# A decoder layer on one core: the same 4459 steps, written out in another order

## The chip, the core and the metric

One core of a Trainium2 chip runs the whole program. It has five engines with a queue each: TensorE (PE, matmuls; its weight loads are listed as PEld), VectorE (DVE), ScalarE (ACT), GpSimd (POOL), and SyncE (SP), which here only issues DMAs. Semaphores order them. The metric is the device time of one execution in microseconds, as the median over runs. Beside it stand times of one profiled execution, in which every instruction has a start and a duration; its span goes from the first to the last instruction.

## The reference

Sixteen samples (`x` is 16 x 512 x 256) go through one decoder layer in float32. Nothing passes from one sample to another.

```python
def attn(h):                      # 16 heads of 16, 64 landmarks
    q, k, v = heads(h @ Wqkv + bqkv);  q = q * scale
    q_l, k_l = mean8(q), mean8(k)      # 8 rows to a landmark
    attn1, attn2, attn3 = softmax(q @ k_l.T), softmax(q_l @ k_l.T), softmax(q_l @ k.T)
    V = attn2
    for _ in range(6):
        KV = attn2 @ V
        V = 0.25 * V @ (13*I - KV @ (15*I - KV @ (7*I - KV)))
    return attn1 @ (V @ (attn3 @ v)) @ Wout + bout
x = x + attn(layernorm(x))
x = x + cross_attention(layernorm(x), ctx, mask)   # 64 keys, 16 heads
h = layernorm(x)
e = argmax(gelu(h[:, -1] @ Wp1 + bp1) @ Wp2 + bp2) # one expert of 8 for each sample
x = x + h + 0.3 * ((gelu(h @ W1[e] + b1[e]) @ W2[e] + b2[e]) @ Wo + bo)
```

(The last line is written as the kernel has it: `h + 0.3 * out` is what the expert layer returns.)

## The kernel before

The work is cut into steps. A step is one engine's share of one operation of one sample, from one to about 30 instructions, with one increment of that engine's semaphore at its end. A word such as `P.jT.1-2` names it: engine (P, A, D, G for POOL, S for SP), kind, part, and how many samples behind the newest one it works. `TURN` lists the steps of one turn; `program()` unrolls it over 16 samples, so that a turn works on four or five samples at once, and `LAST` lists the last steps one by one, with the sample behind `@`. `PROGRAM` is that list. Each engine executes its own steps in the list's order, and waits only for the steps that its data or its buffers need (`unmet`). The eight PSUM banks are given out in the same order (`plan()`): a matmul step takes the bank that has been free longest, and waits for the step that emptied it. So the list alone decides the order on each engine, and which bank each step waits for.

Kinds that matter here:
- `xnTa`, `xnTb`, `xnTc` transpose the normalised input of the three parts; `q`, `k`, `v` project; `s2`, `s3`, `s1`, `t1` are scores of the first attention, `sx`, `tx` of the second; `mx3`, `mx1`, `mxx` their maxima on DVE; `e3`, `e1`, `ex` their exponentials on ACT; `den`, `o`, `w` the sums, the weighted values and the output projection, with `1` or `x` behind; `rec` the reciprocals.
- One of the six rounds of the inverse: PE's `iT` and `iZ` (L1133), from which DVE makes `wb` and ACT `az`; then PE's `jT` and `jZ` (L1143), from which DVE makes `ut` and `uz`, and POOL from `ut` the `b7` for the next `iT`.
- `gate`, `logit`, `exp` choose the expert and load its weights; `h` and `y3` compute it.
- Only once, for sample 0: `w2`, `f` and `fb` multiply each expert's second matrix with the output matrix and store the result; `cn` loads 16 constants; `cst` makes constants on POOL; `kx` computes all keys of the cross attention.

PE works with four shapes of its array: the full 128 x 128 (projections, transposes, experts), 64 x 64 (the inverse and `a`, `x2T`, `y`), 32 rows by 128 columns (all scores), and 128 rows by 32 columns (`den`, `o`, `zT`); `vx` takes 128 by 64. A neighbouring pair of steps in different shapes is called a switch here, and a run of steps in one shape a group.

A wait for a bank and the 64 x 64 matmuls read so:

```python
for j in range(banks_of(step)):
    if BEFORE[i, step, j]:
        who, i0, emptier = BEFORE[i, step, j]
        if c := unmet(pe, who, i0, emptier):
            pe.wait_ge(done[who], c)
```

Of the kernel before, what the change touches and what calls it, by code (L numbers as in the profile page):

```python
# [13 lines left out]
P = 128  # L14
# [16 lines left out]
    D.wb.5.0-3 P.h.2-4 G.kbd-2 D.s2-2 P.jZ.5-3 A.f.2-1 D.uz.5.1-3 D.uz.5.0-3 D.rec1.1.1-3 P.h.1-4 P.y-3
    P.s3.0-2 A.h.2-4 D.y-3 P.o1.0-3 P.o1.1-3 D.rec1.0.1-3 D.o1.0-3 D.o1.1-3 D.mx3.0.0-2 D.mx3.0.2-2
    A.e2-2 P.h.3-4 A.e3.0.0-2 D.mx3.0.3-2 D.mx3.0.1-2 P.w1.1-3 A.e3.0.2-2 D.soft2-2 D.w1.1-3 A.e3.0.3-2
    A.e3.0.1-2 P.w1.0-3 D.w1.0-3 P.f.1-1 P.f.7-2 D.lnB-3 G.xr-2 A.h.1-4 A.f.7-2 S.x-1 G.lnB-3 P.h.0-4
    P.p3T.0-2 P.p3T.3-2 P.p3T.2-2 P.p3T.1-2 A.h.0-4 A.p3T.0-2 A.p3T.1-2 P.x2T-2 S.f.5-3 P.s3.1-2 A.x2T-2
    A.p3T.2-2 A.h.3-4 D.mx3.1.3-2 D.mx3.1.1-2 A.p3T.3-2 P.a.0-2 A.e3.1.3-2 A.e3.1.1-2 P.a.1-2 P.zT.0-2
    D.mx3.1.2-2 D.mx3.1.0-2 P.kx.0-2 P.y3.1-4 A.a.0-2 P.p3T.7-2 P.p3T.5-2 A.e3.1.2-2 A.e3.1.0-2 S.f.1-2
    G.b7.0.0-2 P.p3T.6-2 A.zT.0-2 P.p3T.4-2 P.xnTb.0-3 A.a.1-2 D.lnA-1 G.b7.0.1-2 A.p3T.7-2 S.w2.6-1
    P.xnTb.1-3 D.kx.0-2 A.p3T.5-2 P.f.5-2 A.p3T.6-2 G.x1b-3 A.p3T.4-2 P.fb A.xnTb.0-3 P.s1.0-2
    A.xnTb.1-3 A.f.5-2 D.y3.1-4 P.zT.1-2 P.iT.0-2 A.zT.1-2 D.mx1.0.0-2 S.w2.3-1 P.qx.0-3 G.lnA-1 P.z-2  # L40
    P.f.0-1 S.cn-1 D.mx1.0.2-2 P.f.3-1 D.wb.0.1-2 A.qx.0-3 D.mx1.0.3-2 P.qx.1-3 A.qx.1-3 D.z-2 P.kx.1-2
    D.mx1.0.1-2 D.wb.0.0-2 P.sx.0-3 D.mxx.0.1-3 D.kx.1-2 P.sx.1-3 D.nmA-1 D.mxx.0.3-3 D.mxx.0.0-3
    P.y3.0-4 D.mxx.1.2-3 S.w2.5-1 D.mxx.1.3-3 D.mxx.1.1-3 P.iZ.0-2 A.az.0.0-2 D.mxx.1.0-3 D.mxx.0.2-3
    A.f.1-1 P.xnTa.1-1 A.az.0.1-2 A.xnTa.1-1 A.f.0-1 D.mpx-3 S.f.6-3 P.xnTa.0-1 D.y3.0-4 A.xnTa.0-1
# [30 lines left out]
    A.e1.1.3@14 D.uz.2.1@14 D.lmq.0@15 P.iZ.3@14 A.q.1@15 P.iT.3@14 A.az.3.0@14 D.lmq.1@15 A.az.3.1@14
    P.v.0@15 D.wb.3.0@14 G.qbd@15 D.wb.3.1@14 P.jT.3@14 D.v.0@15 P.jZ.3@14 D.ut.3.0@14 P.s2@15
    D.ut.3.1@14 G.b7.4.0@14 D.uz.3.0@14 D.uz.3.1@14 G.b7.4.1@14 P.s3.0@15 D.s2@15 P.iZ.4@14 D.mx3.0.0@15
    P.iT.4@14 A.az.4.0@14 A.az.4.1@14 P.v.1@15 D.mx3.0.1@15 A.e2@15 D.wb.4.0@14 A.e3.0.0@15 D.wb.4.1@14
    D.mx3.0.2@15 A.e3.0.1@15 P.jT.4@14 D.mx3.0.3@15 P.jZ.4@14 A.e3.0.2@15 D.ut.4.0@14 P.p3T.1@15
    D.ut.4.1@14 G.b7.5.0@14 A.e3.0.3@15 D.uz.4.0@14 P.p3T.0@15 D.uz.4.1@14 P.p3T.2@15 G.b7.5.1@14  # L80
    A.p3T.0@15 D.soft2@15 P.s3.1@15 A.p3T.1@15 A.p3T.2@15 P.iT.5@14 D.mx3.1.0@15 P.den1.1@14 D.wb.5.0@14
    A.e3.1.0@15 D.wb.5.1@14 P.p3T.3@15 D.mx3.1.1@15 P.den1.0@14 A.p3T.3@15 D.mx3.1.2@15 A.e3.1.1@15
    P.iZ.5@14 D.mx3.1.3@15 A.e3.1.2@15 P.p3T.4@15 D.v.1@15 A.az.5.0@14 P.p3T.5@15 D.rec1.0.0@14
    A.az.5.1@14 P.zT.0@15 A.e3.1.3@15 P.jZ.5@14 A.p3T.4@15 D.rec1.1.0@14 P.p3T.7@15 A.p3T.5@15
    P.p3T.6@15 A.zT.0@15 A.p3T.7@15 D.uz.5.0@14 A.p3T.6@15 P.s1.0@15 D.uz.5.1@14 D.rec1.0.1@14 P.y@14
# [1364 lines left out]
```

## Time and profile before

| | |
|---|---|
| median of 3 runs | 1486.27 us (1485.98 to 1490.58) |
| the profiled execution | 1485.77 us, span 1484.1 us |
| mean granted clock of TensorE | 0.987 of full |
| PE busy | 1426.5 us, 96% |
| DVE, ACT, POOL busy | 1009.7, 736.2, 572.1 us |
| share of the last chain on PE | 93% |

The profile's page tells how busy each engine was, and follows the chain of work that ended last.
### The profile page before, as it was taken

To read this page: it belongs to the slowest core of one execution; us is meant where nothing else is said; L and a number is where in the kernel's file an instruction comes from. 1 tells how busy PE (TensorE), PEld (TensorE's weight loads), DVE (VectorE), ACT (ScalarE), POOL (GpSimd) and SP (SyncE) were. 2 spreads that over 40 slices of the span, in tenths; PEclk is the share of its full clock that TensorE was granted. 3 is DMA by queue.
4 is the path that set the end of the run, shared out by engine and by line. 5 is a ranking of instruction groups with operands and counts; after the bars stand their busy time and mean duration, and the time that the engine had idled before them with its cause. 6 is when DMAs were issued, how large, how long until landed. Compare 5 with 4: busy or idle time off the path is not lost.

```text
span 1484.1 us, 51020 instructions
## 1 busy us (share of the span) xinstructions
PE 1426.5 (96%) x22484; PEld 946.3 (64%) x22484; DVE 1009.7 (68%) x2098; ACT 736.2 (50%) x1428; POOL 572.1 (39%) x688
## 2 busy tenths in 40 slices
...
DMA packets 40270, 53.02 MB, mean 36 GB/s; under 512 B 9442, under 2 KB 30194, under 8 KB 40050
## 3 DMA queue, kind: packets, MB, share of 16 engines
...
q8 instruction: 178, 2.92, 0.8%
q14 instruction: 42, 0.34, 0.1%
...
## 4 chain that ended last, share of the span: by engine, by line
PE 93%; DVE 3%; issue 1%; ACT 1%; POOL 1%; DMA 0%; POOLq 0%; DVEq 0%; SPq 0%; ACTq 0%
PE bank L1115 43%; PE bank L1340 8%; PE bank L1133 8%; PE bank L1143 7%; PE bank L1327 5%; PE bank L1227 4%; PE bank L1186 3%; PE bank L1295 2%; PE bank L1207 2%; PE bank L1236 2%; PE bank L1123 2%; PE bank L1308 2%; PE bank L1286 1%; PE bank L1221 1%; PE bank L1213 1%
## 5 line engine op out<-in xcount | busy, mean ns | idle before, releaser
L607 POOL TENSOR_TENSOR b<-ut,eye 128x256 f32<-128x256 f32 x192 | 137.4, 728 | 331.5 <-DVE ut L960 287.4
L765 ACT ACTIVATE az<-bank 128x320 f32<-128x320 f32 x192 | 68.3, 400 | 201.8 <-PE bank L1133 199.6
L1115 PE MATMUL bank<-xnT_c,w1e 128*128 128x512 f32 x256 | 124.9, 615 | 9.0 <-DMA row_e<-w2o_row 7.8
L1016 DVE RECIPROCAL oT_x<-bank 128x256 f32<-128x256 f32 x64 | 107.8, 1725 | 31.9 <-PE bank L1340 31.9
L713 ACT ACTIVATE p<-bank,nm 128x512 f32<-128x512 f32 x128 | 86.8, 690 | 78.8 <-DVE nm L905 78.7
L1115 PE MATMUL bank<-xnT_a,wqkv 128*128 128x512 f32 x256 | 125.6, 614 | 0.0
L1115 PE MATMUL bank<-w2e,hT 128*128 128x256 f32 x512 | 118.4, 385 | 1.6 <-ACT hT L820 1.6
L783 ACT ACTIVATE pT<-bank 128x512 f32<-128x512 f32 x128 | 71.0, 607 | 93.7 <-PE bank L1329 93.6
L1016 DVE RECIPROCAL oT<-bank 128x256 f32<-128x256 f32 x64 | 112.0, 1752 | 2.8 <-PE bank L1340 0.5
L990 DVE TENSOR_REDUCE m<-bank 128x8 f32<-128x512 f32 x128 | 82.5, 685 | 45.8 <-PE bank L1295 44.9
L905 DVE TENSOR_REDUCE nm<-bank 128x1 f32<-128x512 f32 x128 | 79.5, 682 | 43.2 <-PE bank L1207 43.2
L529 POOL TENSOR_TENSOR xr<-x_in,bout_row 128x1024 f32<-128x1024 f32 x16 | 38.0, 2373 | 181.1 <-DVE x L1043 181.1
L1115 PEld LDWEIGHTS bank<-w2e,hT 128*128 128x128 f32 x512 | 94.8, 190 | 19.2 <-ACT hT L820 3.3
L969 DVE SCALAR_TENSOR_TENSOR uz<-uz,bank 128x320 f32<-128x320 f32 x192 | 78.1, 436 | 35.2 <-PE bank L1143 35.2
L951 DVE SCALAR_TENSOR_TENSOR wb<-bank,eye 128x256 f32<-128x256 f32 x192 | 74.2, 416 | 27.3 <-PE bank L1133 26.9
L990 DVE TENSOR_REDUCE m_x<-bank 128x8 f32<-128x512 f32 x128 | 78.2, 682 | 21.4 <-PE bank L1308 21.4
L784 ACT ACTIVATE pT_x<-bank,neg_bias 128x512 f32<-128x512 f32 x128 | 77.2, 689 | 25.3 <-PE bank L1329 25.3
L960 DVE SCALAR_TENSOR_TENSOR ut<-ut,bank 128x256 f32<-128x256 f32 x160 | 61.2, 410 | 41.1 <-PE bank L1143 41.1
L511 POOL TENSOR_SCALAR var_eps_c<-mv_c 128x4 f32<-128x4 f32 x16 | 3.7, 233 | 220.0 <-DVE mv_c L841 220.0
L1133 PEld LDWEIGHTS bank<-uz,ut 64*64 64x64 f32 x3072 | 59.4, 134 | 45.3 <-DVE m L990 10.6
L1143 PEld LDWEIGHTS bank<-az,wb 64*64 64x64 f32 x3072 | 61.0, 135 | 35.4 <-issue 17.0
L1115 PEld LDWEIGHTS bank<-xnT_c,w1e 128*128 128x128 f32 x256 | 45.9, 192 | 58.4 <-issue 44.7
...
## 6 DMA issues: line engine op xcount, KB each, us to landing
...
```

Of the source, the lines that this page charges most:

```text
L607: return g.tensor_tensor(b7[:, q, :], ut[:, q, :], eye[28 if it else 7][:].unsqueeze(1) .broadcast_to([P, 4, LM]), ALU.subtract).then_inc( ...
L713: return s.activation(p3[:, j], tile(i, ("s3", k), j)[:], ACT.Exp, bias=nm3[:, c:c + 1], accum_out=sum3[:, c:c + 1]).then_inc(act_done, 1)
L784: return s.activation(pT[x][:, 4 * k + j, :], src, ACT.Exp, bias=neg_bias[:, i:i + 1]).then_inc(act_done, 1)
L905: return v.tensor_reduce(nm3[:, c:c + 1], tile(i, ("s3", k), j)[:], AX.X, ALU.max, negate=True).then_inc(dve_done, 1)
L969: return v.scalar_tensor_tensor(uz[:, q, lo:], uz[:, q, lo:], 3.25 if it else 13.0, src[:, :, lo:], ALU.mult, ALU.subtract).then_inc(dve_d ...
L990: return v.tensor_reduce(m[x][:, :, j, 2 * k:2 * k + 2], tile(i, ("s" + x, k), j)[:].rearrange("p (t h c) -> p t h c", t=T, h=2), AX.X, AL ...
L1016: return v.reciprocal(oT[x][:, k, half], tile(i, ("den" + x, k))[:, half]).then_inc(dve_done, 1)
L1115: last = mm(dst, lhsT, rhs, start=(k == 0), stop=(k == len(pairs) - 1))
L1133: last = mm(tile(i, step, r)[64 * c:64 * c + 64, w * j + lo:w * j + hi], lhsT[q, j + 4 * c, 0:LM], rhs[q, j + 4 * c, lo:hi], start=True, s ...
L1143: last = mm(tile(i, step, c)[64 * r:64 * r + 64, w * j + lo:w * j + hi], lhsT[q, r, j, 0:LM], rhs[q, r, j, lo:hi], start=True, stop=True)
L1327: mm(tile(i, step, j)[:], flat(keys[rows(j), n]), query[rows(j), n, :], start=True, stop=False)
L1340: last = mm(o[rows(j), :], w, pT[x][:, 4 * n + j, :], start=True, stop=True)
```

## The change

`TURN` and `LAST` are replaced by other lists. Both programs have the same 4459 steps with the same instructions in them; nothing else in the file differs, but that all lines behind the lists stand 44 lines lower. `LAST` had 512 steps, 161 of them on PE, and has 899, 284 of them on PE (a steady turn has 86 on PE). In the costs by which the new lists were drawn up, a switch from the full array to 64 x 64 tiles counts twice as dear as others. The first and the last line of each list, before and now:

```diff
 TURN = """
-    S.fc P.s2-2 P.iZ.5-3 P.iT.5-3 G.cst-2 A.az.5.0-3 G.row-4 D.rec1.1.0-3 A.f.4-2 D.wb.5.1-3 A.az.5.1-3
...
-    D.uz.4.0-2 G.qbd-1 G.b7.5.1-2 D.ut.4.0-2 G.b7.5.0-2 D.uz.4.1-2
+    S.fc A.e3.0.1-3 A.f.7-3 P.w1.0-4 P.h.0-5 A.p3T.0-3 P.p3T.3-3 A.h.1-5 A.h.0-5 D.soft2-3 D.w1.1-4
...
+    D.mx3.0.3-2 A.e3.0.2-2 D.kx.0-2 A.e3.0.3-2 D.mx3.0.1-2 P.p3T.0-2 S.w2.2
 """
 LAST = """
-    A.az.0.1@14 D.y3.0@12 A.xnTa.1@15 P.jT.0@14 D.mx1.1.0@14 S.out@12 P.jZ.0@14 D.ut.0.0@14 P.xnTa.0@15
...
-    P.y3.1@15 D.y3.0@15 D.y3.1@15 S.out@15
+    D.rec1.1.1@12 A.e2@13 P.h.3@11 P.y@12 D.y@12 P.s3.0@13 A.h.3@11 D.rec1.0.1@12 P.o1.0@12 P.o1.1@12
...
+    D.y3.1@15 P.y3.0@15 D.y3.0@15 S.out@15
 """
```

Counted in the two lists, PE's order holds:

| | before | now |
|---|---|---|
| switches in all | 789 | 773 |
| of these full array to 64 x 64 | 178 | 147 |
| groups on the full array, one to each switch away from it | 252 | 232 |
| groups in the other shapes | 537 | 541 |
| switches in one steady turn (full-array groups) | 50 (16) | 49 (15) |

Three places show what moves.

On TensorE (PE), a steady turn, between the cross-attention scores of one sample (`kx_bd,qxT`, L1308) and those of its next sample (`kbd,qT`, L1295); `w2e,hT` is `y3.0`, `ident,xn_a` the two transposes `xnTa`, `uz,ut` is `iZ.0`, `az,wb` and `wb,az` are `jZ.0` and `jT.0`. Before:

```order
L1308 MATMUL bank<-kx_bd,qxT 128x128 x16
L1115 MATMUL bank<-w2e,hT 128x256 x8
L1133 MATMUL bank<-uz,ut 64x80 x16
L1186 MATMUL bank<-ident,xn_a 128x128 x8
L1143 MATMUL bank<-az,wb 64x80 x16
L1143 MATMUL bank<-wb,az 64x64 x16
L1295 MATMUL bank<-kbd,qT 128x128 x16
L1315 MATMUL bank<-ident_bf,m_parts_x 128x128 x4
```

and now:

```order
L1352 MATMUL bank<-kx_bd,qxT 128x128 x16
L1159 MATMUL bank<-w2e,hT 128x256 x8
L1230 MATMUL bank<-ident,xn_a 128x128 x8
L1177 MATMUL bank<-uz,ut 64x80 x16
L1339 MATMUL bank<-kbd,qT 128x128 x16
L1187 MATMUL bank<-wb,az 64x64 x16
L1187 MATMUL bank<-az,wb 64x80 x16
L1359 MATMUL bank<-ident_bf,m_parts_x 128x128 x4
```

The two transposes stand right behind `y3.0` now, so that one group of full-array matmuls takes the place of two, and `s1.1` stands between `iZ.0` and `jT.0`.

On VectorE (DVE), in the first 70 us, with `nm` of `mx3`, `x_in`'s statistics (`lnA` of sample 1), the masks and `kxT` (`kx.0`), and the first maxima of `s1`. Before:

```order
L923 TENSOR_TENSOR attn<-attn,r 128x512
L905 TENSOR_REDUCE nm<-bank 128x1 x4
L838 BN_STATS stats_a<-x_in 128x6 x4
L841 BN_AGGR mv_a<-stats_a 128x2 x4
L1050 TENSOR_SCALAR pT_x<-mask_in 128x1024
L1051 TENSOR_SCALAR neg_row<-mask_in,neg_col 128x1024
L1052 TENSOR_SCALAR neg_bias<-mask_col 128x16
L1058 SCALAR_TENSOR_TENSOR kxT<-bank,bkx_col,pT_x 128x512 x2
L990 TENSOR_REDUCE m<-bank 128x4x2 x2
```

and now:

```order
L949 TENSOR_REDUCE nm<-bank 128x1 x3
L1094 TENSOR_SCALAR pT_x<-mask_in 128x1024
L1095 TENSOR_SCALAR neg_row<-mask_in,neg_col 128x1024
L1096 TENSOR_SCALAR neg_bias<-mask_col 128x16
L1102 SCALAR_TENSOR_TENSOR kxT<-bank,bkx_col,pT_x 128x512 x2
L949 TENSOR_REDUCE nm<-bank 128x1
L963 TENSOR_REDUCE r<-attn 128x8
L965 RECIPROCAL r<-r 128x8
L967 TENSOR_TENSOR attn<-attn,r 128x512
L949 TENSOR_REDUCE nm<-bank 128x1 x4
L882 BN_STATS stats_a<-x_in 128x6 x4
```

`kx.0` stood behind the statistics of sample 1 and right ahead of the maxima of `s1.0`; it stands ahead of both now, between the third and the fourth maximum of `s3.0`.

On SyncE's queue (SP), at the start, behind the loads of the first constants (`bout_row` is the last of them); `pT_x<-in_ctxT` is the first of the 16 loads of `cn`, and `w2o<-hT` the stores `f.0` and `f.1`. Before:

```order
L431 DMA bout_row<-in_bout 128x256
L440 DMA xn_c<-in_W2T 128x2x512
L440 DMA w2e<-in_W2T 128x2x512
L437 DMA pT_x<-in_ctxT 128x2x1024
L437 DMA mask_in<-in_mask 128x1024
```

and now:

```order
L475 DMA bout_row<-in_bout 128x256
L484 DMA x<-in_W2T 128x2x512
L484 DMA xn_c<-in_W2T 128x2x512
L484 DMA w2e<-in_W2T 128x2x512
L484 DMA xnT_c<-in_W2T 128x2x512
L494 DMA w2o<-hT 128x1024
L484 DMA base<-in_W2T 128x2x512
L494 DMA w2o<-hT 128x1024
L481 DMA pT_x<-in_ctxT 128x2x1024
```

All 16 loads of `cn` stand behind the two stores now, which wait for ScalarE's `f.0` and `f.1`; in the order before, the first store stood behind all loads.

Smaller moves inside the turn: in the rounds 2 and 4 of the inverse `iT` now stands ahead of `iZ`, and `jZ.1` now takes one bank that `ex.0.3` on ACT empties, where both of its banks came from `wb` on DVE. On POOL, `cst` stood between `qbd` and `kbd` of sample 0 and now stands ahead of `ksq` and `qbd`.

## Rows read from the trace of the kernel before

**Rows 1.** The page, part 1: PE's busy time, its share of the span, its instructions.
```profile
PE 1426.5 (96%) x22484; PEld 946.3 (64%) x22484; DVE 1009.7 (68%) x2098; ACT 736.2 (50%) x1428; POOL 572.1 (39%) x688
```

**Rows 2.** Windows: busy us of each engine in a stretch, granted clock, DMA share, GB/s.
```profile
400.00:500.00 100.00, 99.19 (x1696) 66.93 (x1692) 74.05 (x157) 50.73 (x98) 36.64 (x42) 1.00 0.09 30
...
1300.00:1400.00 100.00, 93.19 (x1696) 58.07 (x1687) 78.31 (x148) 42.62 (x89) 29.97 (x34) 0.90 0.05 15
1400.00:1484.00 84.00, 66.13 (x356) 42.48 (x354) 26.76 (x61) 25.16 (x41) 21.20 (x19) 0.94 0.14 48
```

**Rows 3.** Timeline of PE, a steady turn: start us, us, group of like instructions.
```profile
633.11 3.62 PE L1115 MATMUL bank<-wout,oT 128*128 128x256 f32 x16
636.56 1.88 PE L1115 MATMUL bank<-xnT_c,w1e 128*128 128x512 f32 x4
...
675.80 1.07 PE L1340 MATMUL bank<-pT_x,ones_bd 128*32 128x512 f32 x8
676.80 1.98 PE L1115 MATMUL bank<-xnT_a,wqkv 128*128 128x512 f32 x4
...
678.94 1.06 PE L1340 MATMUL bank<-pT_x,ones_bd 128*32 128x512 f32 x8
679.82 1.90 PE L1340 MATMUL bank<-pT_x,vx_bd 128*32 128x512 f32 x16
681.65 0.67 PE L1115 MATMUL bank<-wv,ctxT 128*64 128x128 f32 x8
...
690.08 1.99 PE L1115 MATMUL bank<-wqkv,xnT_a 128*128 128x256 f32 x8
692.00 0.69 PE L1143 MATMUL bank<-wb,az 64*64 64x64 f32 x32
```

**Rows 4.** Waits of PE, whole run: us in total, times, longest.
```profile
PE bank L1115 <- DMA row_e<-w2o_row: 7.8, 1, 7.8
PE bank L1327 <- DVE ut L960: 6.3, 12, 0.5
```

**Rows 5.** Timeline of ACT, DVE and PE around 674 us, with idle time ahead.
```profile
672.86 2.42 ACT L784 ACTIVATE pT_x<-bank,neg_bias 128x512 f32<-128x512 f32 x4 [0.96 <-PE bank L1329]
...
673.51 0.75 DVE L960 SCALAR_TENSOR_TENSOR ut<-ut,bank 128x256 f32<-128x256 f32 x2 [0.18 <-PE bank L1143]
...
674.52 1.14 PE L1327 MATMUL bank<-qxT,kx_bd 32*128 32x512 f32 x8 [0.52 <-DVE ut L960]
```

**Rows 6.** Timelines of the head: POOL, SP's issue, DVE, and PE's first wait.
```profile
39.14 0.10 POOL L545 MEMSET neg_col<- 128x1 f32 x1
...
52.16 2.37 POOL L529 TENSOR_TENSOR xr<-x_in,bout_row 128x1024 f32<-128x1024 f32 x1
...
54.62 0.37 SPq L428 DMA_DIRECT2D x_in<-in_x  x1
...
58.93 1.40 DVE L838 BATCH_NORM_STATS2 stats_a<-x_in 128x6 f32<-128x256 f32 x4 [6.53 <-DMA x_in<-in_x]
...
62.63 1.41 DVE L1058 SCALAR_TENSOR_TENSOR kxT<-bank,bkx_col,pT_x 128x512 f32<-128x512 f32 x2 [0.52 <-issue]
...
64.14 1.17 PE L1295 MATMUL bank<-kbd,qT 32*128 32x128 f32 x32 [2.43 <-issue]
```

**Rows 7.** Timelines of the head: SP's first and last constant load, PE at 42 us.
```profile
8.42 0.63 SPq L437 DMA_DIRECT2D pT_x<-in_ctxT  x1
...
21.67 0.29 SPq L437 DMA_DIRECT2D bp_row<-in_bp  x1
...
42.24 3.72 PE L1115 MATMUL bank<-wfo,xnT_c 128*128 128x256 f32 x16
```

**Rows 8.** Windows: DMA after 30 us; both ends of the slow clock late.
```profile
30.00:35.00 5.00, 5.00 (x21) 3.65 (x20) 1.28 (x2) 2.36 (x5) 0.12 (x1) 1.00 0.07 28
...
1371.00:1376.00 5.00, 3.89 (x123) 3.60 (x126) 2.96 (x13) 0.34 (x2) 1.41 (x2) 0.50 0.01 3
...
1386.00:1391.40 5.40, 5.40 (x30) 1.36 (x32) 2.98 (x4) 1.98 (x3) 1.38 (x1) 0.50 0.00 0
```

More of the change, by code:

```diff
@@ L29 @@
 TURN = """
-    S.fc P.s2-2 P.iZ.5-3 P.iT.5-3 G.cst-2 A.az.5.0-3 G.row-4 D.rec1.1.0-3 A.f.4-2 D.wb.5.1-3 A.az.5.1-3
[L31 to L44, printed above, removed]
@@ new lines @@
+    G.lnB-4 A.f.0-2 A.a.1-3 A.e3.1.3-3 P.p3T.6-3 P.p3T.4-3 A.a.0-3 A.p3T.5-3 A.p3T.6-3 A.zT.0-3 P.f.5-3
+    A.p3T.4-3 P.p3T.7-3 P.xnTb.1-4 P.xnTb.0-4 P.s1.0-3 A.f.1-2 G.b7.0.1-3 A.xnTb.1-4 D.lnA-2 G.b7.0.0-3
+    A.f.5-3 S.ctx-3 A.xnTb.0-4 A.p3T.7-3 P.iT.0-3 D.wb.0.1-3 P.zT.1-3 D.y3.1-5 P.qx.0-4 G.lnA-2
+    D.mx1.0.0-3 D.mx1.0.2-3 D.mx1.0.3-3 A.zT.1-3 P.kx.1-3 D.mx1.0.1-3 S.w2.3-2 S.w2.7-2 P.z-3 D.z-3
+    A.qx.0-4 P.qx.1-4 A.qx.1-4 D.wb.0.0-3 D.nmA-2 P.f.3-2 P.sx.0-4 D.mxx.0.0-4 P.sx.1-4 D.mxx.0.2-4
@@ L75 @@
[L75 to L85, printed above, removed]
@@ new lines @@
+    P.h.0@11 P.p3T.3@13 D.w1.1@12 P.p3T.2@13 D.w1.0@12 A.h.1@11 P.p3T.1@13 A.p3T.3@13 A.h.0@11 P.s3.1@13
+    A.p3T.2@13 A.p3T.1@13 D.lnB@12 P.x2T@13 G.xr@13 P.zT.0@13 A.x2T@13 P.a.1@13 P.a.0@13 D.mx3.1.0@13
+    D.mx3.1.2@13 D.mx3.1.1@13 S.x@14 D.mx3.1.3@13 A.e3.1.0@13 P.y3.1@11 D.lnA@14 A.e3.1.1@13 A.e3.1.3@13
+    A.a.1@13 A.a.0@13 A.zT.0@13 A.e3.1.2@13 P.p3T.5@13 G.lnB@12 A.p3T.5@13 P.p3T.6@13 P.p3T.4@13
+    P.xnTb.0@12 P.xnTb.1@12 A.p3T.6@13 P.p3T.7@13 G.b7.0.0@13 G.b7.0.1@13 A.p3T.4@13 A.xnTb.1@12
@@ new lines @@
+    P.s1.0@13 A.p3T.7@13 A.xnTb.0@12 P.iT.0@13 D.wb.0.0@13 D.mx1.0.2@13 G.lnA@14 D.y3.1@11 D.mx1.0.0@13
+    D.mx1.0.1@13 P.zT.1@13 D.wb.0.1@13 P.qx.0@12 P.qx.1@12 A.zT.1@13 D.mx1.0.3@13 A.qx.0@12 P.z@13
+    A.qx.1@12 P.sx.0@12 D.z@13 D.mxx.0.2@12 D.mxx.0.0@12 P.sx.1@12 P.xnTa.0@14 D.mxx.1.3@12 D.mxx.1.2@12
+    D.mxx.1.0@12 D.mxx.1.1@12 A.xnTa.0@14 P.y3.0@11 P.xnTa.1@14 P.iZ.0@13 D.mxx.0.1@12 D.mxx.0.3@12
+    P.s1.1@13 A.az.0.0@13 A.az.0.1@13 D.mpx@12 D.y3.0@11 A.xnTa.1@14 P.jT.0@13 P.jZ.0@13 D.ut.0.1@13
@@ new lines @@
+    D.soft2@14 A.p3T.2@14 D.w1.0@13 P.x2T@14 D.lnB@13 G.xr@14 S.x@15 A.h.0@12 A.h.2@12 A.x2T@14
+    P.zT.0@14 D.mx3.1.1@14 A.e3.1.1@14 D.mx3.1.0@14 G.lnB@13 P.a.0@14 P.a.1@14 D.mx3.1.2@14 D.mx3.1.3@14
+    A.e3.1.3@14 P.p3T.5@14 A.e3.1.2@14 A.a.0@14 A.p3T.5@14 P.y3.1@12 A.e3.1.0@14 A.zT.0@14 P.p3T.6@14
+    A.a.1@14 P.p3T.4@14 A.p3T.6@14 G.b7.0.0@14 G.row@12 P.xnTb.1@13 G.b7.0.1@14 P.p3T.7@14 A.p3T.4@14
+    P.xnTb.0@13 D.y3.1@12 A.xnTb.1@13 A.p3T.7@14 P.s1.0@14 D.lnA@15 A.xnTb.0@13 P.iT.0@14 P.zT.1@14
@@ new lines @@
+    A.az.2.0@14 G.kbd@15 D.lmq.1@15 P.den1.1@14 P.jZ.2@14 D.rec1.1.0@14 P.jT.2@14 P.mTx@13 G.qbd@15
+    D.ut.2.1@14 P.s2@15 A.mTx@13 D.uz.2.1@14 D.ut.2.0@14 D.rec1.1.1@14 P.s3.0@15 G.b7.3.1@14 P.den1.0@14
+    D.uz.2.0@14 P.iZ.3@14 G.b7.3.0@14 D.mx3.0.2@15 A.e3.0.2@15 D.s2@15 D.mx3.0.1@15 A.az.3.1@14
+    P.iT.3@14 A.az.3.0@14 D.wb.3.1@14 P.p3T.2@15 D.wb.3.0@14 A.p3T.2@15 D.mx3.0.0@15 A.e3.0.1@15
+    D.mx3.0.3@15 A.e2@15 P.jT.3@14 D.ut.3.0@14 P.jZ.3@14 A.e3.0.0@15 P.p3T.1@15 D.ut.3.1@14 A.p3T.1@15
```

168 lines of the change are left out of this document (106 added, 62 removed).

## Prediction

> **What bounds the kernel now.** I read the page first, then the windows, then PE's timeline in a steady turn, then PE's waits, and last the two ends. The page shows PE busy for 1426.5 of 1484.1 us [rows 1], so at most 58 us are idle, and no other engine is near. The windows say where: in a steady stretch PE is busy for 99.19 of 100 us, from 1300 to 1400 for 93.19 at a mean clock of 0.90, and in the last 84 us for 66.13 [rows 2]. The middle of the program is thus a stream of matmuls almost without holes. An order can win there only by making the stream itself shorter, and it can lose by opening holes. The two ends have holes, and there the order on the other engines counts.
>
> The stream has a cost that no wait shows, the switch of array shape. The same eight 128 x 256 matmuls appear in two settings. In w1, sixteen of them between other full-array steps take from 633.11 to 636.56, or 1.725 us for eight. As v, between two 64 x 64 steps, eight take from 690.08 to 692.00, or 1.92 [rows 3]. Entering and leaving the full array costs 0.195 us together. For another shape, den and ox (128 by 32, eight matmuls each): entered only, 678.94 to 679.82, 0.88; two behind each other, left only, 679.82 to 681.65, 1.83; entered and left, 675.80 to 676.80, 1.00 [rows 3]. With b for the work, b + entry = 0.88, 2b + exit = 1.83, b + entry + exit = 1.00, so exit 0.12, b 0.855, entry 0.025, and a group of this shape costs 0.145 for its two sides. I take this for the 64 x 64 and 32 by 128 groups too. So a switch away from the full array is no dearer than others: leaving the full array and entering 64 x 64 is about half of a pair, 0.1 to 0.2 us.
>
> **The change, part by part.** *Switches.* There are 20 groups fewer on the full array and 4 more in other shapes (the table of the change). The sum is -20 x 0.195 + 4 x 0.145 = -3.9 + 0.6 = -3.3 us. Of this a steady turn has one full-array group less, about 11 times; the rest lies in the last samples. It counts in full only where PE doesn't wait afterwards for something that its earlier arrival doesn't speed up. As the middle is 99% busy, I keep it whole; the bounds are -3.9, if the other shapes cost nothing, and -1.6, if half is spent in waits near the end.
>
> The Trainium skill's page "TensorEngine Tiling (Array Packing)", section "Key Properties", says that a change of tiling mode drains TensorE, whichever modes; "TensorE: Matmul & The Clock Gate", section "Single matmul latency", puts a drain at about 175 ns. By these the sum would be an estimate of 16 switches x 0.175 = -2.8 us. The rows agree with the drain as such, but price the sides unevenly.
>
> *The wait in the head.* PE stands still for 2.43 us ahead of s1.0 of sample 0 at 64.14, shown as "issue" [rows 6]. What it waits for is a bank that kx.0 on DVE empties: DVE's last instruction of kx.0 starts at 62.63 and takes 1.41, to 64.04 [rows 6]. DVE was late because lnA of sample 1 stands ahead of kx.0, and was idle for 6.53 us until `x_in` landed [rows 6]. The load was late in its turn, issued at 54.62 once xr had ended, and xr began at 52.16 because cst, from 39.14 on, stood ahead of it on POOL [rows 6]. Now kx.0 stands ahead of lnA, and cst behind POOL's first lnA, where POOL has long been idle in wait for `ksum`. Both links of the chain are gone: -2.4 us. The cover is that PE gives kx.0 its matmuls earlier, behind s3.0 at about 42.2 [rows 7]; kx.0 ends on DVE about 1.5 us behind them, at 47.3, while PE is in f.7 to 49.3 and its first dependants are two transposes later. If it were late, mx3.0.1, the softmax behind it and p3T.1 would be next.
>
> *The constants.* SP issues cn from 8.42 to 21.96 before [rows 7]. Now cn stands behind the stores f.0 and f.1. f.1 is stored when its copies on ACT have ended, at about 20 us by my reading (its matmuls come fourth on PE, as f.0's did). So cn begins at about 20.5 and, at the same pace of 13.5 us, ends at 34. The DMA engines are nearly done by 30 before (share 0.07 from 30 to 35 [rows 8]), and the same bytes are to be moved, so I expect the last constant at 34 to 38 us, ahead of the 42.2 at which kx.0 wants it. I cost this at 0; if it fails, PE waits in front of kx.0, by 3 us for a landing at 45.
>
> *The bank of jZ.1.* PE waits 12 times, 0.5 us each and 6.3 in all, for DVE's ut ahead of tx.1 [rows 4]. In the turn shown DVE starts its two `ut` at 673.51 and ends at 674.26, PE starts at 674.52 [rows 5]. Now jZ.1 waits first, for the bank of ex.0.3, the first exponential behind tx.0: ACT starts them at 672.86 and takes 2.42 / 4 = 0.6 for one [rows 5], so the bank is free at 673.5 and jZ.1 starts some 0.4 us late. It still ends at about 674.4, and tx.1 starts at 674.5 as before, when `ut` is done. So the wait changes its place and not its size: 0. If ACT had another step ahead, each 0.1 us would cost 1.2 us over 12 turns.
>
> *iT ahead of iZ.* In round 4 DVE's `wb` starts one step sooner, which could take away part of a wait ahead of jZ.4; but ACT's `az` comes as much later. I take 0, and -1 to +1 us for this and all other exchanges of neighbours in the turn.
>
> *The end.* From the last exponentials on, both orders run the same chain through one sample; its 7.8 us wait for the expert's weights [rows 4] stays. Before that lies a stretch at half clock, from 1371 to 1391.4 (0.50 [rows 8]). PE was not full when it began: 3.89 of 5 us even at that clock. Round 4 and 5 of the last inverse stand there with little between them. The new list has as little between them (iT.4, iZ.4, jT.4 and jZ.4 directly behind each other), so I expect the slow stretch again, and 0 for it.
>
> **The sum.** -3.3 - 2.4 = -5.7 us. The profiled execution took 1485.77 us, 0.5 below the median of the runs. 1486.3 - 5.7 = 1480.6; since the small exchanges lean to the good side (fewer holes in the new head too), I say 1480 us.
>
> **The rivals.**
> *New holes in the turn.* Most steps of PE start a few tenths of a microsecond behind what they wait for. If one dependency per turn comes 0.7 us late (a `b7` on POOL, an exponential), 11 or 12 turns cost 8 us, and the time is 1488. For it: the margin of the stream is under 1%. Against: the places that I followed keep their distances. 0.15.
> *A longer slow clock at the end.* The granted clock fell once when PE had holes [rows 8]. At half clock dense matmuls take twice the time; the 5.4 us window ending it had PE busy throughout [rows 8]. If the new order starts a second stretch of 20 us in dense work, it costs up to 10 us: 1480 + 10 = 1490, slower than before from a stretch of about 13 us more. 0.1. The same page on TensorE, section "What's actually happening", says that the slow clock is the default and activity releases it; the rows agree, and the rule by itself doesn't tell whether the new list idles enough.
> *No slow clock at the end.* If the new list keeps PE busier from 1360 to 1380, the stretch vanishes. In it, PE's dense part, from about 1384 to 1391, would take half: 3.5 us, and the half-filled part before perhaps 2 more. 1480 - 5.5 = 1474.5. 0.2.
> *No gain.* The switches saved are eaten by waits, since everything behind PE must also be ready sooner, and only the head's 2.4 us stay: 1484. 0.2.
> *As forecast*, 1477 to 1483: 0.35.
>
> **The chances.** A measurement of this kernel can tell about 0.3%, 4.5 us. Faster is below 1481.8: the third rival (0.2), two thirds of the forecast case (0.24), and some of the rest, 0.5 in all. Same, up to 1490.7, holds the fourth rival, the remaining third and most of the first: 0.38. Slower needs the second rival, or the first at a higher price: 0.12. The range for 8 in 10 is 1472 to 1489; the forecast's own is 1477 to 1483.
>
> **What the profile should show.** PE's time in a steady turn is shorter by 0.2 us; the wait of 2.43 us in the head is gone, with DVE's kx.0 over before 50 us; waits "ut" ahead of tx.1 turn into waits of jZ.1 for ACT's `pT_x`, with nearly the same sum; SP's cn ends by 35 us; the slow clock near the end has its 20 us. I am wrong if PE's waits in the middle grow by more than 3 us, if PE waits ahead of kx.0, or if the slow clock is granted for another length of time.

## The result, and the profile after

The changed kernel takes 1473.83 us (median of 6 runs, 1471.28 to 1478.28), the kernel before took 1485.62 beside it (6 runs, 1484.54 to 1490.58). The ratio is 0.9921, with a 95% interval of 0.9901 to 0.9942: faster by 11.8 us. The forecast was 1480, with 1472 to 1489 as range. The profiled execution has a span of 1469.5 us and a mean granted clock of 0.993.

The page of the changed kernel, part 1 and one row of part 3 (DMA queue: transfers, MB, share):

```profile
PE 1423.0 (97%) x22484; PEld 946.0 (64%) x22484; DVE 1018.0 (69%) x2098; ACT 738.3 (50%) x1428; POOL 570.7 (39%) x688
...
q8 instruction: 178, 2.92, 0.8%
```

PE is busy for 3.5 us less than in [rows 1] and idle for 11 us less. The second row is needed below: 178 times in the run, 16 KB of instructions are fetched. They are PE's: between two fetches lie 256 of PE's matmuls and weight loads on average. The kernel before has the same row.

Where the time went is best read at one step that stands once in each sample, `s2`. PE's timeline of the kernel before, samples 2 and 13:

```profile
185.24 1.13 PE L1213 MATMUL bank<-ksq,qbd 128*128 128x256 f32 x4
...
1143.85 1.13 PE L1213 MATMUL bank<-ksq,qbd 128*128 128x256 f32 x4
```

and of the changed one:

```profile
183.92 1.13 PE L1257 MATMUL bank<-ksq,qbd 128*128 128x256 f32 x4
...
1134.15 1.13 PE L1257 MATMUL bank<-ksq,qbd 128*128 128x256 f32 x4
```

Up to sample 2 the change gains 1.3 us. The 11 samples from 2 to 13 take 958.6 us before and 950.2 now, 8.4 less. What follows takes 340.2 and 335.4 in these two executions. So most of the gain lies in the turn, where the forecast had put about 2 us. The turns are the firm part of this count. The 1.3 us ahead of them are within what executions differ: kernels with the old head reach the same `s2` of sample 2 at 185.24, 186.65 and 187.07 us.

The same steps of two steady turns, from `y3.0` to `tx.1`, as PE's timeline shows them. Before:

```profile
573.68 3.72 PE L1115 MATMUL bank<-w2e,hT 128*128 128x256 f32 x16
577.33 0.78 PE L1133 MATMUL bank<-uz,ut 64*64 64x80 f32 x32
578.04 1.09 PE L1186 MATMUL bank<-ident,xn_a 128*128 128x128 f32 x8
579.09 0.78 PE L1143 MATMUL bank<-az,wb 64*64 64x80 f32 x32
...
585.94 0.69 PE L1143 MATMUL bank<-wb,az 64*64 64x64 f32 x32
586.45 0.73 PE L1143 MATMUL bank<-az,wb 64*64 64x80 f32 x32
587.71 0.71 PE L1327 MATMUL bank<-qxT,kx_bd 32*128 32x512 f32 x4 [0.52 <-DVE ut L960]
```

and now:

```profile
570.38 3.72 PE L1159 MATMUL bank<-w2e,hT 128*128 128x256 f32 x16
573.93 1.04 PE L1230 MATMUL bank<-ident,xn_a 128*128 128x128 f32 x8
574.90 0.78 PE L1177 MATMUL bank<-uz,ut 64*64 64x80 f32 x32
575.61 1.17 PE L1339 MATMUL bank<-kbd,qT 32*128 32x128 f32 x32
...
582.55 0.69 PE L1187 MATMUL bank<-wb,az 64*64 64x64 f32 x32
583.40 0.78 PE L1187 MATMUL bank<-az,wb 64*64 64x80 f32 x32 [0.15 <-ACT pT_x L828]
584.21 0.71 PE L1371 MATMUL bank<-qxT,kx_bd 32*128 32x512 f32 x4
```

`y3.0` and the two `xnTa` take 3.65 + 1.05 us before (573.68 to 577.33, 578.04 to 579.09) and 4.52 now (570.38 to 574.90): 0.18 less, since they are one group. From `jT.1` to `tx.1` it is 1.77 before and 1.66 now.

The largest single part is the wait ahead of `jZ.4` (`az,wb`), behind `den1.0` (`pT,ones_bd`). Before, and then now:

```profile
617.08 1.07 PE L1340 MATMUL bank<-pT,ones_bd 128*32 128x512 f32 x8
618.34 0.78 PE L1143 MATMUL bank<-az,wb 64*64 64x80 f32 x32 [0.19 <-DVE wb L951]
...
613.49 1.07 PE L1384 MATMUL bank<-pT,ones_bd 128*32 128x512 f32 x8
614.53 0.78 PE L1187 MATMUL bank<-az,wb 64*64 64x80 f32 x32
```

From start to start it is 1.26 us before and 1.04 now.

I laid all 86 steps of PE in the undisturbed turns side by side, by the starts of their last matmuls. Such a turn takes 86.56 us before and 86.12 now, 0.44 less. The parts: the merged group -0.17, `jT.1` and `jZ.1` -0.11, the wait ahead of `jZ.4` -0.21, two smaller ones -0.10, the step from `s2` to `iZ.5` +0.15. Eleven times 0.44 is 4.8 of the 8.4 us. The other 3.6 are in single turns: before, samples 2, 3, 7, 8 and 10 take 87.6 to 88.0 us and one 86.8, now three are 0.5 to 0.8 us longer than an undisturbed one and two 0.3 to 0.4. In the five long turns of before, and in the three longest now, PE stands still in front of a matmul that waits for nothing that the trace shows, its word for this being "issue".

The head, on SP, DVE and PE (the first and last load of `cn`, `kx.0`, and `s1.0` of sample 0):

```profile
21.61 0.43 SPq L481 DMA_DIRECT2D pT_x<-in_ctxT  x1
...
31.96 0.29 SPq L481 DMA_DIRECT2D bp_row<-in_bp  x1
...
47.23 1.41 DVE L1102 SCALAR_TENSOR_TENSOR kxT<-bank,bkx_col,pT_x 128x512 f32<-128x512 f32 x2
...
62.84 1.17 PE L1339 MATMUL bank<-kbd,qT 32*128 32x128 f32 x32
```

The wait of 2.43 us in [rows 6] is gone: from `s2` of sample 0 to `s2` of sample 1 it takes 60.9 us in place of 63.4. Ahead of that this execution is 1.25 us late, `s2` of sample 0 starts at 41.46, before at 40.21. The whole delay lies in PE's second step, `f.2`, which takes 5.66 us in place of 4.30. The new order isn't shown to be the reason: in kernels with the old head `f.2` takes 4.30 to 5.65 us.

The end, in windows as in [rows 8], one of the stretch of slow clock and one behind it:

```profile
1366.80:1370.10 3.30, 3.29 (x44) 1.56 (x48) 0.43 (x2) 1.86 (x2) 2.79 (x2) 0.50 0.60 192
1371.00:1376.00 5.00, 4.45 (x88) 2.55 (x92) 0.66 (x4) 4.98 (x10) 2.43 (x3) 1.00 0.22 77
```

The slow clock lasted 3.4 us there, not 20.5.

### The profile page after: what moved, and what is told of

It is laid out like the page before. It is cut to its first block, busy times and chain, and to the rows that moved or that the text cites. A ratio compares the mean times of both kernels' runs of the same rounds, so it can differ in the third digit from the quotient of the medians.

```text
span 1469.5 us, 50951 instructions
## 1 busy us (share of the span) xinstructions
PE 1423.0 (97%) x22484; PEld 946.0 (64%) x22484; DVE 1018.0 (69%) x2098; ACT 738.3 (50%) x1428; POOL 570.7 (39%) x688
## 4 chain that ended last, share of the span: by engine, by line
PE 92%; DVE 3%; ACT 2%; issue 1%; DMA 1%; POOL 1%; SPq 0%; POOLq 0%; DVEq 0%
PE bank L1159 43%; PE bank L1384 8%; PE bank L1177 7%; PE bank L1187 6%; PE bank L1371 5%; PE bank L1271 4%; PE bank L1230 3%; PE bank L1339 2%; PE bank L1251 2%; PE bank L1280 2%; PE bank L1167 2%; PE bank L1352 2%; PE bank L1330 1%; PE bank L1265 1%; DMA row_e<-w2o_row 1%
## 5 line engine op out<-in xcount | busy, mean ns | idle before, releaser
L827 ACT ACTIVATE pT<-bank 128x512 f32<-128x512 f32 x128 | 74.3, 602 | 93.2 <-PE bank L1373 93.0
L864 ACT ACTIVATE hT<-bank,b1e 128x512 f32<-128x512 f32 x64 | 42.3, 686 | 81.7 <-PE bank L1159 81.5
L768 ACT ACTIVATE p3T<-bank 128x512 f32<-128x512 f32 x128 | 71.7, 604 | 22.4 <-PE bank L1271 21.9
```

The source lines that it names most:

```text
L827: return s.activation(pT[x][:, 4 * k + j, :], src, ACT.Exp).then_inc(act_done, 1)
```

## The experiments

Beside each stands the kernel before on the same chip (1485.45 to 1485.49 us). The ratios are given as they were recorded, each with its 95% interval; they are not exactly the quotients of the two medians.

**The two lists apart.** First the new `TURN` with the old `LAST`, then the old `TURN` with the new `LAST`.

> The new TURN with the old LAST. Theory (gains add up by place): the head and the steady turns bring what they brought in the changed kernel, 9.7 us by the start of s2 of sample 13, and the end is as before with its slow clock of about 20 us: 1476 us. Rival (the end decides, the turn only shifts waits): the gain up to sample 13 is given back in the old end, and the time is within 3 us of 1485.6.

Measured: 1472.93 us (1470.41 to 1474.73), ratio 0.9918 (0.9904 to 0.9932). The new `TURN` alone brings the whole gain. Against the kernel before, its profiled execution gains 2.6 us up to `s2` of sample 2, 7.8 up to sample 13, and 2.8 behind it, 13.2 in all. Its slow clock at the end is still long:

```profile
1361.50:1378.20 16.70, 15.49 (x179) 7.41 (x179) 5.28 (x16) 8.34 (x13) 3.07 (x3) 0.50 0.22 72
```

> The old TURN with the new LAST. Theory: up to sample 11 nothing changes, and the new end brings 4.8 us, since the slow clock is granted for about 3.4 us in place of 20.5: 1481 us. Rival (the slow clock hangs on where in time the end falls, not on its order): 10 to 20 us of slow clock remain and the time is 1484 to 1487 us.

Measured: 1484.63 us (1481.58 to 1487.55), ratio 0.9992 (0.9981 to 1.0003). The stretch of slow clock is gone from its place:

```profile
1360.00:1395.00 35.00, 30.35 (x689) 18.25 (x688) 26.68 (x55) 19.11 (x34) 16.16 (x20) 1.00 0.11 36
```

and yet the time is the same, the interval reaching down to 2.8 us less. From `s2` of sample 15 to the end it takes 177.4 us (before 183.9), from sample 13 to 15 it takes 162.7 (before 156.3): in this execution what is won behind is given back ahead. The new `LAST` by itself isn't the reason for that, since the changed kernel, with the same list, takes 156.1 us from 13 to 15. In the execution of this kernel, slow spells of 3.4 us stood elsewhere, one of them at 1151 and one at 1240, and beside them three standstills of 0.8 to 1.4 us; why they came there is open.

**The head's wait.** Two ways to take it away alone: on DVE

```diff
-D.lnA-1 ... D.kx.0-2
+D.kx.0-2 D.lnA-1
```

> The kernel before with one step moved: DVE's kx.0 ahead of its lnA of sample 1. Theory: the wait of 2.43 us ahead of s1.0 of sample 0 is gone, and s2 of sample 1 starts at 101.2 us in place of 103.6; the time is 1483.2. Rival: PE waits for something else there (kbd or the transposed p3), and less than 1 us is won.

and on POOL

```diff
-... P.iT.5-3 G.cst-2 A.az.5.0-3 ... G.ksq-1
+... P.iT.5-3 A.az.5.0-3 ... G.cst-1 G.ksq-1
```

> The kernel before with one step moved: POOL's cst ahead of ksq of sample 0, where POOL is idle. Theory: xr ends some 12 us earlier, x_in of sample 1 is issued at about 43 in place of 54.6, lnA is done before kx.0's matmuls are, and the same 2.43 us are gone without a change on DVE: 1483.2. Rival: cst pushes ksq and qbd back and s2 of sample 0 starts later than at 40.2 us, which eats the gain.

Measured: 1482.66 (ratio 0.9977, 0.9967 to 0.9987) and 1482.69 (0.9981, 0.9971 to 0.999), against 1485.48. PE's `s1.0` of sample 0 in the first kernel:

```profile
59.70 2.10 PE L1115 MATMUL bank<-wfo,base 128*128 128x256 f32 x9
61.74 1.17 PE L1295 MATMUL bank<-kbd,qT 32*128 32x128 f32 x32
```

It starts at 61.74, 2.4 us sooner than in [rows 6], and without a wait; in the second kernel at 61.69. So the chain was as the prediction read it, and undoing either of its two links is enough.

**The merged group, taken out of the new order.** The changed kernel with `iZ.0` ahead of the two `xnTa` again:

```diff
-P.xnTa.1-2 P.xnTa.0-2 ... P.iZ.0-3
+... P.iZ.0-3 P.xnTa.1-2 P.xnTa.0-2
```

> The changed kernel with the two transposes xnTa moved back behind iZ.0, which gives each turn its second full-array group again. Theory A (the merged group is worth what the prediction priced, 0.195 us in each turn): a steady turn of 86.12 + 0.17 to 0.20 = 86.30 us, and about 11 to 15 x 0.19 = 2 to 3 us in all, 1476 us. Theory B (the turn's gain is in shorter waits, and the group is worth nothing because a wait behind it takes it up): a steady turn within 0.05 us of 86.12. Rival C (the groups carry the whole gain of the turn): 86.56 again, and 1480 us.

Measured: 1486.04 us (1481.74 to 1490.77), ratio to the kernel before 1.0002 (0.999 to 1.0014). All theories missed it: with this one exchange 12 us are lost, which is the whole gain. The undisturbed turn is 86.80 us, 0.67 longer. Between the two profiled executions lie 14.4 us, and the turns are about half of them: 7.6 from `s2` of sample 2 to 13. 2.8 lie ahead (0.74 of them a new wait of PE in front of `k.0` of sample 0, for ACT's copy of `xnTa`), and 4.0 behind, where the slow clock lasted 10.2 us in place of 3.4. The PE timeline of the turn:

```profile
580.21 0.79 PE L1177 MATMUL bank<-uz,ut 64*64 64x80 f32 x32
580.93 1.09 PE L1230 MATMUL bank<-ident,xn_a 128*128 128x128 f32 x8
582.47 1.17 PE L1339 MATMUL bank<-kbd,qT 32*128 32x128 f32 x32 [0.45 <-ACT xnT_a L722]
```

0.15 us are the two array switches that come back (`y3.0` 3.65 for 3.56 us, `xnTa.1` 0.49 for 0.44). The other 0.52 are nearly all a wait. `s1.1` takes four banks, and one of them is emptied by ACT's copy of `xnTa.1`. In the new order `iZ.0` lies between them too and covers the copy; here only the short `xnTa.0` does.

**Small moves in the old order.** DVE's `mp1` behind `ut.1.0`; `iT.4` ahead of `iZ.4`; and five moves together (the two head moves, both of these, and the two `xnTa` ahead of `iZ.0`).

```diff
-P.jT.1-2 D.mp1-2 P.jZ.1-2 A.ex.0.1-3 D.ut.1.1-2 D.ut.1.0-2
+P.jT.1-2 P.jZ.1-2 A.ex.0.1-3 D.ut.1.1-2 D.ut.1.0-2 D.mp1-2
```

> The kernel before with DVE's mp1 moved behind ut.1.0, so that the two instructions of ut.1 no longer stand behind it. Theory A (tx.1's wait for ut was a wait for mp1 ahead of it): the PE wait for ut ahead of tx.1 falls below 1 us in all, jZ.1 or jT.1 waits for ACT's exponentials instead, a steady turn is 0.11 us shorter (86.45), and the time 1.3 us shorter (1484). Theory B (as the prediction had it, the wait only changes its place): a steady turn of 86.56 and no change of time.

Measured: 1485.39 us, ratio 1.0004 (0.9994 to 1.0013), the turn 86.56 us, the wait for `ut` ahead of `tx.1` as long as before. `ut` doesn't wait for `mp1`, it waits for PE's `jT.1` ([rows 5] have it so). Theory A fell.

```diff
-P.iZ.4-2 P.iT.4-2
+P.iT.4-2 P.iZ.4-2
```

> The kernel before with iT.4 ahead of iZ.4 and nothing else moved. Theory A (DVE's wb.4 then starts one step sooner and lies hidden by den1.0, so that jZ.4 finds it ready): a steady turn 0.21 us shorter (86.35), the time 2.5 us shorter (1483). Theory B (as the prediction had it: az comes as much later as wb comes sooner): a steady turn within 0.05 us of 86.56. Rival C: iT.4 has to wait for b7.4 on POOL, which now is one step closer, and the turn is longer by up to 0.3 us.

Measured: 1490.84 us, ratio 1.0029 (1.0018 to 1.004), the turn 86.98 us, 0.43 longer. PE's timeline of round 4:

```profile
616.44 1.98 PE L1115 MATMUL bank<-xnT_a,wqkv 128*128 128x512 f32 x4
618.50 0.69 PE L1133 MATMUL bank<-b,uz 64*64 64x64 f32 x32
618.99 0.76 PE L1133 MATMUL bank<-uz,ut 64*64 64x80 f32 x32
619.68 1.06 PE L1340 MATMUL bank<-pT,ones_bd 128*32 128x512 f32 x8
621.21 0.78 PE L1143 MATMUL bank<-az,wb 64*64 64x80 f32 x32 [0.46 <-ACT az L765]
```

`iT.4` comes 0.15 us late behind `q.1` (2.06 us from start to start, 1.91 before), as rival C had it, and `jZ.4` waits 0.46 us for ACT's `az`, where it waited 0.19 for `wb` before. In the old list an exponential, `e1.1.0`, stands between ACT's two `az.4`; in the new one it doesn't.

> The kernel before with five small moves together: kx.0 ahead of lnA on DVE and cst ahead of ksq on POOL (the head), mp1 behind ut.1.0, iT.4 ahead of iZ.4, and the two xnTa ahead of iZ.0. Theory A (the gain of the new order is the sum of these): the head 2.4 us shorter, the steady turn 0.17 + 0.11 + 0.21 = 0.49 us shorter (86.07), 12 times that or 5.9 us, so 1485.5 - 8.3 = 1477 us, and the rest of the new turn's gain (to 1473) is what the slow clock and the stalls shown as issue do. Theory B (the moves don't add up, since each wait taken away uncovers the next): a steady turn of 86.3 or more and 1480 us or more.

Measured: 1497.44 us, ratio 1.0084 (1.0071 to 1.0097), the turn 87.85 us. In addition to what `iT.4` costs there is this, where `iZ.0` and `jZ.0` now stand behind each other:

```profile
580.76 0.79 PE L1133 MATMUL bank<-uz,ut 64*64 64x80 f32 x32
582.52 0.79 PE L1143 MATMUL bank<-az,wb 64*64 64x80 f32 x32 [0.97 <-ACT az L765]
```

The merged group itself gave 0.17 us here too (`y3.0` -0.093, `xnTa.1` -0.055, `xnTa.0` -0.024). But in the old order the two transposes were the cover under which ACT makes `az.0`, and without them `jZ.0` waits 0.97 us.

**The exchanges with their companions.** If cover and companions are what was missing, they can be moved along:

```diff
-P.y3.0-4 ... P.iZ.0-2 A.az.0.0-2 ... P.xnTa.1-1 A.az.0.1-2 A.xnTa.1-1 ... P.xnTa.0-1 ... A.xnTa.0-1 P.jZ.0-2 P.jT.0-2 ... P.s1.1-2
+P.y3.0-4 ... P.xnTa.1-1 P.xnTa.0-1 P.iZ.0-2 ... A.xnTa.1-1 A.xnTa.0-1 A.az.0.0-2 ... A.az.0.1-2 ... P.s1.1-2 ... P.jZ.0-2 P.jT.0-2
-D.logit-3 D.ut.3.1-2 D.uz.3.1-2 ... P.iZ.4-2 P.iT.4-2 ... A.e1.1.0-2 ... A.az.4.0-2
+D.ut.3.1-2 D.uz.3.1-2 D.logit-3 ... P.iT.4-2 P.iZ.4-2 ... A.az.4.0-2 A.e1.1.0-2
```

> The kernel before with two exchanges of the turn made whole, each with its companions. Place 1: the two xnTa ahead of iZ.0, s1.1 behind iZ.0 in their place as cover for az.0, and ACT's xnTa copies ahead of its az.0. Place 2: iT.4 ahead of iZ.4, ACT's e1.1.0 behind both az.4 instead of between them, DVE's logit behind ut.3 and uz.3. Theory A (the turn's gain comes from whole exchanges, and four_edits lost only because the cover and the companions were missing): from y3.0 to jZ.0 0.17 us less in each turn, den1.0 back from 1.53 to 1.05 us, q.1 at 1.91 instead of 2.06, so a steady turn of 86.56 - 0.17 - 0.21 = 86.18 us and 1485.5 - 12 x 0.38 = 1481 us. Theory B (each change of a bank's owner makes a wait elsewhere, and only the whole new list fits together): one of the two places shows a wait of 0.3 us or more again, the turn is 86.5 or longer, and the time 1485 or more.

Measured: 1491.03 us (1487.15 to 1494.53), ratio 1.0037 (1.0023 to 1.0051), the turn 87.06 us. The two large waits are gone (`q.1` 1.91 us again, `den1.0` to `jZ.4` 1.14, where it was 1.26 before and 1.53 with `iT.4` alone). Of theory B the turn and the time came true, but not a wait of 0.3 us: four new losses of 0.16 to 0.21 us stand further on, behind `jT.0`, `mTx`, `iT.1` and `jT.4`. Two of them in PE's timeline:

```profile
583.66 0.64 PE L1143 MATMUL bank<-wb,az 64*64 64x64 f32 x32
584.45 0.40 PE L1315 MATMUL bank<-ident_bf,m_parts_x 128*128 128x128 bf16 x4
...
622.25 0.67 PE L1143 MATMUL bank<-wb,az 64*64 64x64 f32 x32
623.05 1.07 PE L1340 MATMUL bank<-pT,ones_bd 128*32 128x512 f32 x8
```

From start to start these are 0.79 and 0.80 us; the same two steps of the kernel before take 0.60 each.

**An attempt to better the new turn.** The step from `s2` to `iZ.5` waits for DVE's `uz.4.0`, ahead of which stands a reciprocal of 1.76 us. New `TURN`, old `LAST`, and:

```diff
-D.rec1.0.0-3 P.jT.4-3 ... D.uz.4.0-3
+P.jT.4-3 ... D.uz.4.0-3 D.rec1.0.0-3
```

> The new TURN with the old LAST, and DVE's rec1.0.0 (a reciprocal of 1.76 us) moved behind uz.4.0, for which iZ.5 waits. Theory A (the 0.15 us that the new turn lost at s2 and iZ.5 are the wait for DVE, which the reciprocal holds up): the step from s2 to iZ.5 0.15 us shorter, a steady turn of 85.97 us, and 1472.9 - 1.8 = 1471 us. Theory B (the reciprocal, coming later, holds up o1.0 or wb.5 in turn): a steady turn of 86.1 or more, and 1473 us or more.

Measured: 1480.83 us, ratio 0.9976 (0.9965 to 0.9988), 8 us more than without the move; the turn 86.61 us, 0.49 longer, which is 5.4 in eleven. The place itself gained its 0.15 us. DVE's and PE's timelines of the same turn show what it cost:

```profile
619.33 3.36 DVE L1016 RECIPROCAL oT<-bank 128x256 f32<-128x256 f32 x2
622.61 0.69 DVE L951 SCALAR_TENSOR_TENSOR wb<-bank,eye 128x256 f32<-128x256 f32 x2
...
620.89 1.98 PE L1115 MATMUL bank<-xnT_c,w1e 128*128 128x512 f32 x4
623.45 0.66 PE L1143 MATMUL bank<-az,wb 64*64 64x16 f32 x32 [0.57 <-DVE wb L951]
```

Both reciprocals now stand ahead of `wb.5`, and `jZ.5` waits for it: +0.64.

**The standstills shown as issue.** The kernel before has six of them between `s2` of samples 2 and 14; each begins 1.1 to 2.0 us behind the start of an instruction fetch (the DMA records of the trace on the queue named `q8 instruction`), always in the stretch from `jT.4` to the step behind `iT.5`, the last two rounds of the inverse. Five of the six fetches took 0.90 to 0.95 us, no longer than the median of 0.99 of all, so a slow transfer isn't what they share. To move the places of the fetches and nothing else, 50 waits that are already satisfied go ahead of PE's first one:

```diff
+            for _ in range(50):
+                pe.wait_ge(started, 1)
             if first(pe, pool_consts, 1):
                 pe.wait_ge(pool_consts, 1)
```

(`started` is raised by POOL's fourth `memset`.)

> The kernel before with 50 waits put ahead of PE's first one, on a semaphore that POOL has raised by then; they lie in the 5.6 us in which PE waits anyway, and only move the places in PE's instruction stream at which its next 16 KB are fetched. Theory A (the standstills of PE shown as issue near s2, 0.4 to 1.65 us each and 7.9 us in all, come from where such a fetch falls against the dense 64 x 64 groups): the steady turn stays 86.56, the standstills move to other samples (from samples 2, 3, 8, 9, 11, 13 to about 6, 7, 9, 11), their sum changes, by my reading of the pattern to about 5.4 us, and the time to 1483 us. Theory B (they belong to the order of the steps, or to the transfers of these samples): they stay with the same samples and the time is 1485.5 us.

Measured: 1483.41 us (1481.3 to 1486.75), ratio 0.9986 (0.9977 to 0.9994). The undisturbed turn is 86.56 us to the last digit. But the long turns are others: 2, 6, 7, 8 and 12, in place of 2, 3, 7, 8, 10 and 13. The fetches stand in each sample about where the kernel before has them one sample later, and the loss of sample 7 (0.25 us at `iZ.5` and 1.23 at `den1.1`) stands in sample 6 with the same two numbers. What the samples from 2 on have over the undisturbed turn falls from 8.1 to 5.1 us, and the time by 2.1. Sample 10 in the kernel before, and the same steps with the 50 waits (in lines that stand 3 lower):

```profile
967.85 0.22 PE L1143 MATMUL bank<-wb,az 64*64 64x64 f32 x1
968.90 0.69 PE L1143 MATMUL bank<-wb,az 64*64 64x64 f32 x31 [0.84 <-issue]
```

```profile
967.79 0.67 PE L1146 MATMUL bank<-wb,az 64*64 64x64 f32 x32
968.39 1.06 PE L1343 MATMUL bank<-pT,ones_bd 128*32 128x512 f32 x8
```

Once more with the kernel of the late reciprocal, and 64 waits instead of 50:

> As the kernel with rec1.0.0 late (new TURN, old LAST), with 64 waits ahead of PE's first one as above. If the standstills shown as issue hang on where the fetches fall: those of samples 2 and 3 (0.9 and 1.9 us in the run of the new TURN) are gone or moved, and the time is 0 to 2.5 us below that of the kernel without the 64 waits, 1469 to 1471 us; if they hang on the order or the sample, both kernels take the same.

Measured: 1478.35 us (1476.26 to 1480.92), ratio 0.9952 (0.9938 to 0.9965), 2.5 us less than without them (1480.83), the difference that the first alternative allowed, at a time 7 to 9 us above its forecast. The profiled pair doesn't explain it: the losses beyond the undisturbed turn moved (with the waits nearly all is in sample 2), but their sum over samples 2 to 12 rose from 1.7 to 2.8 us. So this pair bears out that the standstills move, and not what they cost.

## Why the prediction was right, and for what reasons it wasn't

The forecast had the sign and the range right, and 6 us of the size wrong: it had half of the gain. The head's mechanism was right; of the turns' 8.4 us it had the 2 that the merged group gives. That the time fell inside the range owes something to luck, since the 3 us of fewer standstills were in no step. By its own steps:

*Switches, -3.3.* The price per group nearly holds: 0.195 us was priced for a full-array group less, and 0.15 to 0.17 was measured in four kernels. How it divides between entering and leaving, and whether a switch to 64 x 64 is dearer than others, no run tested. The Trainium skill's "TensorEngine Tiling (Array Packing)", section "Key Properties", says that a change of mode drains TensorE. Merging the groups in the old order took two changes out and gave 0.17 us; with the 175 ns for a drain behind a single matmul that the Trainium skill's "TensorE: Matmul & The Clock Gate", section "Single matmul latency", gives, an estimate for two changes would be 0.35. The measurement decides: about 0.09 a change. In the turn the term is worth 11 x 0.17 = 1.9 us. The rest of it was laid into the last samples, and there the new list brought 0.9 us with the old `TURN` (0.9992, an interval that holds 1) and none with the new one (1473.83 for 1472.93).

*Small exchanges in the turn, 0 (-1 to +1).* This step failed. Together with the bank of `jZ.1` they brought another 0.27 us in each turn, 2.9 in eleven: -0.21 ahead of `jZ.4`, -0.11 and -0.10 elsewhere, +0.15 behind `s2`. For `iT.4` the prediction weighed `wb` sooner against `az` later and looked at PE's order alone. Shown by experiment: the exchange alone costs 0.43 us a turn, and with ACT's exponential behind `az.4` and DVE's `logit` behind `uz.3` both of its waits are gone and 0.11 us of the 0.21 are won. Which of the two companions does it was not separated. The bank of `jZ.1` went nearly as told: `jZ.1` waits first, starts 0.34 us late (0.4 was forecast), and `tx.1` follows 0.11 us sooner, not at the same distance. What gives the 0.11 stays open; `mp1` doesn't. The rows leave one lead that no run tests: before, PE's last wait ahead of `tx.1` is for the bank of `ex.0.0` and stands behind that for `ut`, and `tx.1` starts 0.26 us after `ut` has ended; now the wait for `ut` is the last, and it is 0.14. The prediction's sign, that the waits keep nearly the same sum, failed: the wait for `ut` was 6.3 us in all, that of `jZ.1` for ACT's `pT_x` is 1.7. Such sums don't tell what a turn gains, which is 0.11 us.

*The head, -2.4.* Right, and shown by two kernels (2.8 us each). In the profiled execution of the changed kernel only half of it is seen at `s2` of sample 1 (102.37 against 103.60), because `f.2` took longer; from `s2` of sample 0 on all 2.5 us are there.

*The constants, 0.* Right: issued from 21.61 to 32.25 (20.5 to 34 forecast), `kx.0` over on DVE at 48.64 (47.3 forecast), with no wait for them on PE.

*The end, 0, the slow clock again.* The clock was wrong for this execution (3.4 us in place of 20), by the prediction's own list a sign of being wrong, and the zero was right. Nor did the clock fall only once before: it was slow at 108 us too, for 6.8, and at 1456 for 10.2. "No slow clock at the end" gave 1474.5 us, which is nearly the measured time, and it isn't the reason: the new `TURN` with 17.1 slow microseconds takes 1472.93, and the new `LAST` with none at that place takes 1484.63.

*What no step held.* The instruction fetches. The sum over samples 2 to 12 beyond the undisturbed turn is 6.5 us before, 2.9 in the changed kernel and 3.5 with the new `TURN` alone. It isn't the chance of one execution: the four other kernels that share the old turn's 86.56 us and have no waits added have 6.3 to 7.4, the three variants of the new turn 1.7 to 3.0. That the standstills move with the fetches is shown by the 50 waits; why the new order meets fewer of them isn't. The page before had them as "issue", and the prediction took them for the stream's own pace.

The sum that the runs give for the new `TURN`, in the profiled pair: 2.6 up to sample 2 (in the main the head's wait of 2.4, less a standstill of 0.8 at 72.6 us, and 1.5 between samples 1 and 2, where the slow clock lasted 3.4 us in place of 6.8), 4.8 for eleven turns, 3.0 for fewer standstills among them, and 2.8 behind sample 13 (of it 1.65 one standstill), 13.2 us; the medians say 12.6.

"New holes in the turn", which had 0.15, didn't come in the new list. But each smaller version of the turn's change ran into just that: `iT.4` alone, the merged group alone, both with their companions, and the late reciprocal.
